# TensorE's order inside an attention step: the weighing behind score 3, the second maximum between scores 2 and 3

## The reference

```
attn = softmax(q k^T * scale, axis=-1)           # 16 heads, 1024 x 1024 each
attn = attn + rel_bias_table[i - j + 1023]       # 511 rows; larger indices take the last
out  = layernorm(attn @ v) * gamma + beta
```

## Time and profile before

| what | value |
|---|---|
| median of 3 runs | 698.76 us (696.7 to 701.05) |
| the profiled execution's own time | 697.31 us |
| its span | 695.5 us |
| granted TensorE clock over the span | 0.988 |
| TensorE (PE) busy | 605.9 us, 87% |
| VectorE (DVE) busy | 523.9 us, 75% |
| ScalarE (ACT) busy | 376.3 us, 54% |
| GpSimd (POOL) busy | 95.6 us, 14% |
| weighing, L1501 | 1024 instructions, mean 604 ns; 16% of the chain that ended last |
| scores, L1487 | 512, mean 385 ns; 10% of the chain |
| exponentials, L776 | 512, mean 604 ns; waited 115.7 us for scores |
| maxima reduced, L1079 | 256, mean 1,218 ns; waited 33.1 us for TensorE |
| maxima filled, L1421 | 512 instructions, mean 383 ns |

### The profile page before, as it was taken

One profiled execution on the slowest core, in us unless ns is written; L12 is line 12 of the kernel. 1 busy time (PEld: TensorE's weight loads), 2 busy tenths in 40 slices (PEclk: granted clock), 3 DMA queues, 4 the chain that ended last, 5 costly groups with the idle time before them and its releaser, 6 DMA issues.

```text
span 695.5 us, 9222 instructions
## 1 busy us (share of the span) xinstructions
PE 605.9 (87%) x3304; PEld 236.9 (34%) x3304; DVE 523.9 (75%) x958; ACT 376.3 (54%) x692; POOL 95.6 (14%) x96
## 2 busy tenths in 40 slices
PE   7888899899988788888898898888889888887997
PEld 5353545444464542122121121211212112224443
DVE  5657678855769887997978979998998984419734
ACT  3935133333402136776767767787777878762331
POOL 5941120101032802002010000000000011002000
PEclk9999999999999999999999999999999999999999
DMA  8000000000311223003010010010100000000011
GB/s 255 18 1 0 1 0 1 0 1 0 105 60 56 69 66 111 1 22 95 3 36 18 3 52 3 11 46 2 39 16 2 1 2 1 1 1 0 1 30 30
DMA packets 18990, 20.22 MB, mean 29 GB/s; under 512 B 3969, under 2 KB 12673, under 8 KB 18945
## 3 DMA queue, kind: packets, MB, share of 16 engines
q1 hardware_dynamic: 17552, 18.84, 8.7%
q0 software_dynamic: 144, 0.52, 0.2%
q10 hardware_dynamic: 1248, 0.27, 0.2%
HBM read 15.23 MB, written 4.19 MB: 28 GB/s over the span
## 4 chain that ended last, share of the span: by engine, by line
PE 55%; DVE 21%; ACT 11%; SPq 4%; issue 3%; DMA 3%; DVEq 2%; POOL 1%; POOLq 0%; ACTq 0%
PE banks L1501 16%; PE banks L1487 10%; ACT arena L776 8%; DVE negmax L1079 8%; PE banks L1214 6%; PE banks L1292 5%; PE banks L1421 4%; PE banks L1283 3%; SPq L464 3%; PE banks L1335 3%; PE banks L1227 2%; DMA arena<-nm_part 1%; DVE arena L986 1%; PE banks L1436 1%; ACT arena L766 1%
## 5 line engine op out<-in xcount | busy, mean ns | idle before, releaser
L776 ACT ACTIVATE arena<-banks 128x512 f32<-128x512 f32 x512 | 267.7, 604 | 115.9 <-PE banks L1487 115.7
L1079 DVE TENSOR_REDUCE negmax<-banks 128x2 f32<-128x1024 f32 x256 | 299.0, 1218 | 35.3 <-PE banks L1421 33.1
L1487 PE MATMUL banks<-arena 59*128 59x512 bf16 x512 | 139.0, 385 | 31.1 <-ACT arena L776 26.2
L1501 PE MATMUL banks<-arena 128*32 128x512 f32 x1024 | 136.3, 604 | 7.9 <-ACT arena L776 6.6
L1421 PE MATMUL banks<-arena 56*128 56x512 bf16 x512 | 109.7, 383 | 18.9 <-DVE negmax L1079 14.5
L1487 PEld LDWEIGHTS banks<-arena 59*128 59x128 bf16 x512 | 34.3, 93 | 206.9 <-ACT arena L776 183.6
L524 POOL TENSOR_TENSOR rstd<-veps,neghalf 128x4 f32<-128x4 f32 (+1 forms) x24 | 27.1, 1129 | 280.3 <-DVE veps L847 234.9
L1292 PE MATMUL banks<-arena,bT 128*128 128x512 f32 x128 | 60.1, 593 | 1.6 <-ACT arena L619 1.6
L619 ACT ACTIVATE arena<-banks 128x512 f32<-128x512 f32 (+1 forms) x56 | 32.1, 595 | 49.2 <-PE banks L1227 19.2
L933 DVE TENSOR_SCALAR arena<-banks,bi 128x512 f32<-128x512 f32 x32 | 23.9, 745 | 33.1 <-PE banks L1292 33.1
L1421 PEld LDWEIGHTS banks<-arena 56*128 56x128 bf16 x512 | 25.8, 94 | 41.0 <-DVE negmax L1079 34.7
(11 more groups left out here) (145 smaller groups left out, 635.6 us busy)
## 6 DMA issues: line engine op xcount, KB each, us to landing
arena<-qk_scratch SPq DMA_DIRECT2D x128, 48.0 KB
arena<-in_tab SPq DMA_DIRECT2D x4, 1024.0 KB, 6.1
qk_scratch<-arena SPq DMA_DIRECT2D x8, 384.0 KB, 2.6
arena<-qk_scratch SPq DMA_DIRECT2D x64, 16.0 KB
out<-x SPq DMA_DIRECT2D x4, 256.0 KB, 2.3
arena<-nm_part SPq DMA_DIRECT2D x48, 4.0 KB, 1.7
x<-in_x POOLq DMA_DIRECT2D x1, 512.0 KB, 7.7
x<-in_x ACTq DMA_DIRECT2D x1, 256.0 KB, 3.8
```

The lines of the kernel that those rows point to most:

```text
L776: act.activation(probs[s % 2][:, h, :], score_bank(g, n), ACT.Exp, scale=SCALE).then_inc(exp_done, 1)
L1079: return dve.tensor_reduce(negmax[:, buf, keys, :, at_tile], slot, axis=AXX, op=ALU.max, negate=True)
L1487: pe.matmul(score_bank(g, n), ks[rows, g % BUFS, pair, t * P:(t + 1) * P], qs[rows, g % BUFS, pair, q * HALF:(q + 1) * HALF], start=True, ...
L1501: last = pe.matmul(pv_bank[32 * h:32 * h + VW, :], vpg[:, g % BUFS, t, h, :], probs[s % 2][:, h, :], start=t == 0, stop=t == NT - 1)
```

## The change

The weighing of step s - 1 stood between the first ring item and scores 2 and 3. Now it stands behind score 3. The second ring item stood behind score 3; now it stands between scores 2 and 3. Third items of a step stay last, now directly behind the weighing.

```diff
--- before.py
+++ after.py
@@ -1504,18 +1504,21 @@
 
             def step(G, g, s, fill_item, ring):
 
+                def weigh_before():
+                    if s:
+                        weigh(G, g, s - 1)
+                    elif not (isinstance(G, int) and G == 0):
+                        weigh(G - 1, g - 1, STEPS - 1)
+
                 scores(G, g, s, 0)
                 scores(G, g, s, 1)
                 if len(ring) > 0:
                     fill_item(ring[0])
-                if s:
-                    weigh(G, g, s - 1)
-                elif not (isinstance(G, int) and G == 0):
-                    weigh(G - 1, g - 1, STEPS - 1)
                 scores(G, g, s, 2)
-                scores(G, g, s, 3)
                 if len(ring) > 1:
                     fill_item(ring[1])
+                scores(G, g, s, 3)
+                weigh_before()
                 for k in ring[2:]:
                     fill_item(k)
```

## The result

The changed kernel takes **691.93 us** (median of 4 runs, 689.76 to 693.71) against 698.96 us (median of 4 runs as well, 696.7 to 701.05). The ratio is 0.9899, with a 95% interval from 0.9857 to 0.9941. The forecast was 689.7 us, by a sum of -8.5 us; measured are -7.0 us.

The account below looks back on a forecast made before the run. No engine is full in a plain attention round, so a loop between engines was taken to set the pace. The terms summed to -8.5 us, giving 688.8 to 690.3, stated as 689.7 us, range 684 to 698.5.

Parts of the forecast that it names:

- A: The forecast itself: whole kernel at 686 to 694 us, chance 0.62.
- 47 ordinary steps: Attention steps with two maxima and nothing else: 2.40 us instead of 2.61, a gain of 0.21 each, -9.9 us.
- 15 steps with the copy: Steps where ScalarE copies the weighed sum, twice a group: 3.08 us against 3.05, no gain, +0.4 us.
- six turned results: Eight transposes of a group's result, now behind the weighing, delay the second maximum: loss 0.53 + 0.34 each, +5.2 us.
- the bias: Two steps with the bias product in each of the first four rounds: 6.87 us against 7.52, -2.6 us.
- the turned maxima in them: In the bias rounds, a third item behind the weighing loses 0.8, two later ones gain 1.0: together -0.8 us.
- three pieces of the next stage: Last group: the next stage's transposes and two other pieces now stand between a weighing and the next scores, +2.0 us.
- the last piece: Score 3 to weighing in an ordinary step's loop: taken as 0.32 us, bounded by 0.23 and 0.53.
- The switch of shapes: Way out of the bias product's tiling mode, 0.09 us twice in four rounds: 0.7 us, sum -7.8 rather than -8.5.
- B: Rival: fills behind the weighing find their banks free, the 5.2 and 2.0 us fall away: 683 us, chance 0.08.
- C: Rival: gain halved, ordinary step 2.53 instead of 2.40 us: 699 us, half of it 694; chance 0.23.
- D: Rival: VectorE does not catch up behind the result, third maxima or bias: slower, 713 us, chance 0.07.

Follow-up runs that it names:

- e6_wait_added: The kernel before with one more, long-met wait on ScalarE ahead of each exponential 2: 704.75 us, ratio 1.0089.
- e5_one_wait_again: Second run of the changed kernel without ScalarE's wait for the weighing of step s - 2 ahead of exponential 0: 694.17 us, ratio 0.9887.
- e8_third_one_wait: e4_third_ahead with ScalarE's wait for the weighing of step s - 2 ahead of exponential 0 also taken out: 682.97 us, ratio 0.9767.
- e4_third_ahead: The changed kernel with the third items of a step ahead of the weighing instead of behind it: 685.25 us, ratio 0.9804.
- e2_only_weigh: The changed kernel with the second maximum moved behind the weighing, so only the weighing's place differs from the kernel before: 705.77 us, ratio 1.0126.
- the best order: Against the changed kernel, each step reordered: score 0, first maximum, score 1, second maximum, score 2, third items, weighing, score 3: 676.73 us, ratio 0.9683.

## Why the prediction was right

The likeliest case, A, came out: the time lies in 686 to 694 us, and every kind of step has the sign that was worked out. Only sizes were off. The forecast also drew a line at 691.8 us, below which it called the kernel faster, with 0.60 for that: 691.93 lies just above it, too near to decide. The terms, measured in the attention of the two profiles:

| term | forecast | measured |
|---|---|---|
| 47 ordinary steps | -9.9 | -7.4 (0.155 to 0.16 each) |
| ordinary steps of the last group | -1.5 | -1.0 |
| 15 steps with the copy | +0.4 | +0.9 |
| six turned results | +5.2 | +4.2 |
| the bias, four rounds | -2.6 | -3.7 |
| the turned maxima in them | -0.8 | -0.7 |
| start | +1.3 | +1.3 |
| three pieces of the next stage | +2.0 | +1.8 |
| the last two weighings | -1.4 | -1.4 |
| smaller ones (steps 11, the end of group 6) | -1.2 | -1.0 |
| one more wait for landed maxima | none | +0.5 |
| sum | -8.5 | -6.5 |

Part of the agreement is luck: terms that came out worse than forecast sum to some 4.3 us (mainly ordinary steps, last group, copy, landed maxima), and better ones to 2.3 (result, bias, next stage) take half of that back.

- *Ordinary steps.* The walk took 0.42 us from score to exponential, from an exponential behind one wait. Exponential 0 stands behind two, and takes 0.48. This is the mis-sized term, 0.05 to 0.06 us over some 60 steps. The kernel before had shown it where exponential 0 is released by its own score: 449.71 - 449.23 = 0.48, behind the transposes of the earlier trace rows. e6_wait_added shows the 0.06 as an effect of a second wait, and e5_one_wait_again and e8_third_one_wait give it back. The bound on the last piece, from score 3 to the weighing, was not needed: it is 0.32, as taken.
- *The copy.* In the first half of a group it stands behind two waits as well: 1.19 for 1.13.
- *The turned result.* VectorE began to read 1.13 us behind the start of the transposes, not 1.25, and these started 1.00 and not 1.1 behind the weighing: so 3.58 for 3.78. The 1.25 of the earlier trace rows was not the way from TensorE to VectorE but VectorE's own queue: it was still busy with a maximum of 1.23 us that it had begun at 448.32, and had no idle time ahead of the reciprocal at 449.46. In the changed kernel it had waited 1.06 us (444.13). The mechanism, a fill that waits ahead of score 3 and the weighing, is in the rows, and e4_third_ahead takes it away. The maximum at 448.32, from the kernel before:

```profile
448.32 1.23 DVE L1079 TENSOR_REDUCE negmax<-banks 128x2 f32<-128x1024 f32 x1 [0.69 <-PE banks L1421]
```

- *The bias.* The product handed on to score 2 after 265.77 - 263.48 = 2.29 us, a bit more than the 2.18. But score 2 and the second maximum cost 266.01 - 265.77 = 0.24 and not 0.43, since the maximum starts beside the score; so the first step is 4.15 and not 4.25. The transposes of step two cost the loop only 2.45 in all where 2.62 was taken.
- *The switch of shapes.* The Trainium skill (TensorEngine Tiling (Array Packing), Key Properties) says that a change of the tiling mode drains TensorE. The forecast named 0.09 us for a way out of the bias product by that rule, beside its sum. Start to start, the product hands on after 2.18 us to a weighing and after 2.29 to a score, in each of the four rounds: 0.11 more, so in this place the trace agrees with the rule. That a drain makes up the 0.11 isn't shown. And the -7.8 us by that rule, in place of -8.5, didn't come from the bias: its steps gained more than the walk had, 3.7 us and not 2.6.
- *Rivals.* B needed the special steps to be free: they cost 4.2 and 1.8. C had an ordinary step at 2.53: of the 0.13 us that it adds, 0.05 came. D needed VectorE to stay late. It was in time again one step after each result, as the walk had it, and its wait fell.

The medians differ by 7.0 us, 0.5 more than the attention does. The stretch ahead of it, which no edit here touches, takes 251.6 to 255.5 us in the profiles (that at a clock of 0.75 left out).

What stays open: why several runs of e5_one_wait_again and e8_third_one_wait had lower clocks than those of the kernels with both waits, and so how much of the shorter steps a median keeps.

## What to carry to other kernels

Where several engines hand work around in a loop, write the loop down as starts from the timeline: each hop of it is a distance between two rows. Then put on each in-order engine only what the loop needs between its hops, and the rest where that engine waits anyway. A piece that stands directly behind the longest instruction of the loop is paid in full, one ahead of its wait is not: between e2_only_weigh and the changed kernel that difference was worth 13 us, and the best order 23 us against the kernel before, with no instruction less. Moving half of a pair of edits can have the other sign (+6 for the weighing alone).

## What the runs showed that I had not expected

- Here an activation behind two semaphore waits starts 0.06 us later than one behind a single wait, even when the other was met before: 0.48 against 0.42 us from score to exponential, 1.19 against 1.13 to the copy, and +5.4 us when added to one instruction in each of some 126 steps. A wait that program order on the other engine implies is worth taking out of such a loop: it shortened the steps from 2.45 to 2.39 us.
- Parts of an execution ran at a granted clock of 0.51 for 10 us (e5_one_wait_again, 259 to 269 us), with eight products of a weighing taking 1.93 us instead of 1.07. In the 3.8 us before the clock fell, from the first score on, TensorE was busy 2.64 us; in the same stretch of the changed kernel it was busy 2.63 us, and the clock stayed at 1.00. One of the 53 executions of the eight experiments ran at 0.75 throughout, 777 us long.
- A walk over measured distances gave the times of orders never run before: 676 forecast and 676.7 us measured, 683 and 685.2. For e2_only_weigh it gave 0 to 5 us more than before; 6.3 was measured.
